# Rotary projection of the L2a attention on one core: one projection with a partner shuffle in place of two projections

## The chip, the core and the metric

The kernel runs a whole four-block decoder as one program on one core of a Trainium2 chip. The time is device microseconds of one execution, the core's first to last instruction and what lies around it. The kernel before takes 2980.1 us (median of three runs, 2977.56 to 2994.86). Most executions of a kernel agree within 0.3%, about 9 us here.

## The reference

The input `x` has 8 batches of 256 tokens with 128 features. Twelve layers are added to it one after the other: an attention, a cross attention and a feed-forward for each of four blocks. The change is in the attention code that three of them share (L0a, L2a, L3a), and above all in L2a, the only one with a rotary embedding:

```python
def _rotate_half(x):
    x1, x2 = jnp.split(x, 2, axis=-1)
    return jnp.concatenate((-x2, x1), axis=-1)

def _L2_attn_ref(x, Wq, Wkv, Wo, bo):          # 16 heads of 64, 4 key/value heads
    q = (x @ Wq).reshape(b, n, HEADS, DIM_HEAD).transpose(0, 2, 1, 3)
    kv = (x @ Wkv).reshape(b, n, 2 * KV_HEADS, DIM_HEAD)
    k = kv[:, :, :KV_HEADS].transpose(0, 2, 1, 3)
    v = kv[:, :, KV_HEADS:].transpose(0, 2, 1, 3)
    ...
    q = q * cos + _rotate_half(q) * sin
    k = k * cos + _rotate_half(k) * sin
    k = jnp.repeat(k, g, axis=1)
    v = jnp.repeat(v, g, axis=1)
    dots = jnp.einsum('bhid,bhjd->bhij', q, k) * SCALE
    attn = jax.nn.softmax(dots, axis=-1)
    out = jnp.einsum('bhij,bhjd->bhid', attn, v)
    return out.transpose(0, 2, 1, 3).reshape(b, n, HEADS * DIM_HEAD) @ Wo + bo
x = x + _L2_attn_ref(_layernorm(x, axis=-1), ...)
```

So each of the 64 values of a head needs its partner, the value 32 places away, to be rotated.

## The kernel before

`attention_rows` computes L0a, L2a and L3a. All numbers are fp32. In L2a one batch is one **pass** of eight **units** (0 to 7), and a unit is one chunk of two heads: queries and keys lie transposed, the 64 dimensions of two heads on the 128 partitions, the 256 tokens along a row (`qT`, `kT`).

A unit does, for its two heads, *scores* (PE, into `ps_s`), *max* (VectorE, `top`), *exp* (ScalarE, `probs`, four instructions of 128x256 each with a read of its accumulator), and then for earlier chunks: *turn* of the chunk before (PE transposes into `ps_p`, copied to SBUF as `probsT` by ScalarE in L2a), *inverse* of the chunk before (a small reciprocal on VectorE, widened by GpSimd into `wide`), and, for the chunk two before, *spread* (PE transposes `wide`, ScalarE copies it), *values* (PE, into `ps_o`) and *outputs* (VectorE multiplies `ps_o` by `spread` into `oT`).

Beside these, a pass makes the queries and keys of the next batch. The table `slots` says which of these **items** lie in which unit, those of the first list right after *max*, those of the second right after *inverse*. The items are the transposed input x, the queries q and keys k, the values v, the output projection y of the batch before, and the layer norm of the batch after next (ln, ln_rest). One function builds one list, `order`, from the table, and each engine walks through that same list in order and issues its part of each entry. No scheduler moves anything. All items share two PSUM banks (`ps_m`, `m_banks=2`) in turn: PE may start an item only when the item two before it has been taken out of its bank. *Scores* go round three banks (`s_banks=3`), so those of a unit wait until the first head of the unit before has been exponentiated.

A q or k item of L2a makes one chunk (8 q and 2 k items a pass). PE (line 1423) projects twice, with `w_q` and with `w_qr`, whose columns are those of `w_q` with the halves of each head exchanged, so that the partners come to lie on the same partition in the second half of the bank. VectorE (line 1301) multiplies the bank by cos and signed sin in one instruction of 128x512 into a ring of three (`turned`); GpSimd (line 1265) adds the halves into `qT` or `kT` in one instruction of 128x256. *Scores* of a batch's chunk 0 wait for all q and k items of the batch; those of later chunks have no such wait. The weights of L2a are loaded on the SyncE queue during the layer before.

Before the first pass, the same `order` runs eight units in which only items for batch 0 exist (the **prologue**). The last pass has no q, k, x or v items.

## Time and profile before

| | |
|---|---|
| time, median of three runs | 2980.1 us |
| time of the profiled execution | 2979.73 us |
| span of the profiled execution | 2977.9 us |
| PE busy over the span | 2342.9 us (79%) |
| VectorE busy | 1606.9 us (54%) |
| ScalarE busy | 1307.4 us (44%) |
| GpSimd busy | 727.4 us (24%) |
| mean granted TensorE clock | 0.861 of full |

The whole span is an average over twelve layers with different limits, so the shares of the span say little about one of them. L2a lies between 1553.6 us (its first VectorE work starts) and 1894.4 us (its last addition to `x_sb` ends). A row of the timeline gives the start of a run of like instructions, their length together, the engine, the line, the operation and the tiles; behind it, in brackets, the idle time of the engine before it and what ended that.

### The profile page before, as it was taken

How to read it: one execution, taken by the hardware profiler on the slowest of the kernel's cores; microseconds unless marked ns; L12 is line 12 of the kernel's file. 1: busy time of each engine (PE TensorE's matmuls, PEld its weight loads, DVE VectorE, ACT ScalarE, POOL GpSimd, SP SyncE). 2: the span in 40 equal slices, each digit the busy share in tenths (PEclk: the TensorE clock that was granted, in tenths of full speed). 3: DMA queues.
4: the chain of work that ended last, by engine and by line, in shares of the span. 5: the costliest groups of instructions: out<-in, count | busy, mean ns of one | idle time of the engine just before them, and what ended most of it. 6: DMA issues, size and time to landing. Idle time of an engine off the chain costs nothing. (4 is left out here: it accounts for less than half of the span.)

```text
span 2977.9 us, 49335 instructions
## 1 busy us (share of the span) xinstructions
PE 2342.9 (79%) x16238; PEld 1536.2 (52%) x16238; DVE 1606.9 (54%) x4943; ACT 1307.4 (44%) x3187; POOL 727.4 (24%) x1023
## 2 busy tenths in 40 slices
PE   6868985658887389882569999878839996899958
PEld 4624443635544244441457777557727774455533
DVE  4657772135555577753215555453337674877623
ACT  4615552124455145554426666432316553355522
POOL 0132212153332421200563332124231112222000
PEclk9969995858888578995789999988969998899979
DMA  2022224210000022213250000224410001222100
GB/s 72 2 78 83 82 58 148 46 51 29 29 29 15 30 87 74 79 32 99 71 110 1 1 1 1 75 86 150 133 44 2 1 2 39 88 77 77 37 16 14
DMA packets 130876, 160.29 MB, mean 54 GB/s; under 512 B 22581, under 2 KB 93110, under 8 KB 129478
## 3 DMA queue, kind: packets, MB, share of 16 engines
q1 hardware_dynamic: 116008, 132.90, 14.8%
q0 software_dynamic: 12016, 23.19, 3.2%
q8 instruction: 126, 2.06, 0.3%
q10 hardware_dynamic: 2624, 1.31, 0.3%
q14 instruction: 102, 0.83, 0.1%
HBM read 120.77 MB, written 36.68 MB: 53 GB/s over the span
## 5 line engine op out<-in xcount | busy, mean ns | idle before, releaser
L725 DVE CUSTOM_DVE_ANT_0 L3x_ps_ring<-L3x_ps_ring,L3x_mask_q 128x512 f32<-128x512 f32 x256 | 173.9, 708 | 65.9 <-PE L3x_ps_ring L960 51.5
L728 DVE TENSOR_REDUCE L0x_mx<-L0x_ps_ring 128x1 f32<-128x512 f32 x256 | 166.6, 685 | 70.6 <-PE L0x_ps_ring L960 69.5
L728 DVE TENSOR_REDUCE L1x_mx<-L1x_ps_ring 128x1 f32<-128x512 f32 x256 | 166.2, 685 | 61.9 <-PE L1x_ps_ring L960 61.1
L856 ACT ACTIVATE L3x_p_ring<-L3x_ps_t 128x1024 f32<-128x1024 f32 x128 | 131.1, 1025 | 144.4 <-PE L3x_ps_t L999 144.2
L856 ACT ACTIVATE L1x_p_ring<-L1x_ps_t 128x1024 f32<-128x1024 f32 x128 | 130.4, 1025 | 122.6 <-PE L1x_ps_t L992 121.8
L856 ACT ACTIVATE L0x_p_ring<-L0x_ps_t 128x1024 f32<-128x1024 f32 x128 | 130.4, 1025 | 106.8 <-PE L0x_ps_t L992 106.3
L1368 ACT ACTIVATE L2a_probs<-L2a_ps_s,L2a_top 128x256 f32<-128x256 f32 x256 | 118.0, 473 | 93.2 <-DVE L2a_top L1318 92.3
L992 PE MATMUL L3x_ps_t<-L3x_q_stack,L3x_k_stack 75*128 75x256 bf16 x512 | 123.9, 278 | 5.5 <-ACT L3x_p_ring L856 5.4
L960 PE MATMUL L1x_ps_ring<-L1x_k_stack,L1x_q_stack 72*128 72x512 bf16 x256 | 104.0, 431 | 29.7 <-DVE L1x_mx L728 16.1
L960 PE MATMUL L0x_ps_ring<-L0x_k_stack,L0x_q_stack 72*128 72x512 bf16 x256 | 103.2, 428 | 28.8 <-DVE L0x_mx L728 15.5
L999 PE MATMUL L3x_ps_t<-L3x_mask_k,const_ident_bf 128*128 128x256 bf16 x512 | 123.6, 277 | 0.0
L1368 ACT ACTIVATE L3a_probs<-L3a_ps_s,L3a_top 128x128 f32<-128x128 f32 (+1 forms) x256 | 104.2, 423 | 38.9 <-DVE L3a_top L1314 36.7
L960 PE MATMUL L3x_ps_ring<-L3x_k_stack,L3x_q_stack 72*128 72x512 bf16 x256 | 96.9, 410 | 21.1 <-DMA L3x_k_stack<-L3x_k_dram 11.6
L1318 DVE TENSOR_REDUCE L2a_top<-L2a_ps_s 128x2 f32<-128x512 f32 x128 | 82.1, 683 | 18.9 <-PE L2a_ps_s L1447 18.8
L1314 DVE CUSTOM_DVE_ANT_0 L3a_ps_s<-L3a_ps_s,const_causal_min 128x128 f32<-128x128 f32 (+1 forms) x256 | 83.8, 389 | 11.4 <-PE L3a_ps_s L1447 11.4
L1423 PE MATMUL L2a_ps_m<-L2a_xT,kept_a 128*128 128x256 f32 x320 | 88.8, 405 | 1.0 <-ACT L2a_xT L1357 1.0
L1265 POOL TENSOR_TENSOR L2a_qT<-L2a_turned 128x256 f32<-128x256 f32 x64 | 47.2, 737 | 171.9 <-DVE L2a_turned L1301 171.7
L1259 POOL COPY L3a_wide<-L3a_inverse 128x128 f32<-128x128 f32 x128 | 34.0, 295 | 225.0 <-DVE L3a_inverse L1331 225.0
L992 PE MATMUL L0x_ps_t<-L0x_q_stack,L0x_k_stack 75*128 75x256 bf16 x512 | 84.5, 292 | 5.6 <-ACT L0x_p_ring L856 5.6
L992 PE MATMUL L1x_ps_t<-L1x_q_stack,L1x_k_stack 75*128 75x256 bf16 x512 | 84.2, 291 | 5.6 <-ACT L1x_p_ring L856 5.6
L1032 PE MATMUL L1x_ps_o<-L1x_p_ring,L1x_v 128*32 128x256 f32 x1024 | 78.4, 430 | 9.2 <-ACT L1x_p_ring L856 5.5
L1032 PE MATMUL L0x_ps_o<-L0x_p_ring,L0x_v 128*32 128x256 f32 x1024 | 79.2, 434 | 5.5 <-ACT L0x_oT L863 2.1
(681 smaller groups left out, 6097.3 us busy)
## 6 DMA issues: line engine op xcount, KB each, us to landing
L0x_k_stack<-L0x_k_dram SPq DMA_DIRECT2D x96, 96.0 KB
L1x_k_stack<-L1x_k_dram SPq DMA_DIRECT2D x96, 96.0 KB
L3x_k_stack<-L3x_k_dram SPq DMA_DIRECT2D x96, 96.0 KB
L0f_w<-L0f_in_w SPq DMA_DIRECT2D x32, 256.0 KB, 7.0
L1a_rk_wide<-L1a_rk_dram SPq DMA_DIRECT2D x8, 1024.0 KB, 4.8
L1f_w<-L1f_in_w SPq DMA_DIRECT2D x32, 256.0 KB, 3.1
kept_x<-ctxT SPq DMA_DIRECT2D x24, 256.0 KB, 3.2
L0x_q_stack<-L0x_q_dram SPq DMA_DIRECT2D x96, 48.0 KB
```

The lines of the kernel that those rows point to most:

```text
L725: dve.tensor_tensor_reduce(bank, bank, mask_q[:, qt, :], 1.0, 2 * MASKED, ALU.add, ALU.max, accum_out=mx[:, qt, h:h + 1]).then_inc(took_se ...
L728: dve.tensor_reduce(mx[:, qt, h:h + 1], bank, AX, ALU.max).then_inc(took_sem(n), 1)
L856: act.activation(pr, pt, ACT.Exp, scale=scale).then_inc(exp_done.sem, 1)
L960: last = pe.matmul(out, queries[:, t * P:(t + 1) * P], keys[:, 0:seen_keys], start=True, stop=small or not masked)
L992: last = pe.matmul(out, keys[:, t * P:(t + 1) * P], queries[:, q0:q0 + nq], start=True, stop=small and not masked)
L999: last = pe.matmul(out, const["ident_bf"][:], mask_k[:, par if mask_each else 0, t, q0:q0 + nq], start=False, stop=True)
L1032: last = pe.matmul(outputs(g, par)[rows, 0, q0:q0 + nq], val, prob, start=(i == 0), stop=(i == len(pieces) - 1), skip_group_check=True)
L1265: pool.tensor_tensor(dst, part[:, 0, :], part[:, 1, :], ALU.add).then_inc(rotated, 1)
L1314: last = dve.tensor_tensor_reduce(span, span, const["causal_min"][:, S - keys_of(t):S], 1.0, -2 * MASKED, ALU.add, ALU.min, accum_out=top[ ...
L1318: dve.tensor_reduce(top[:, slot, j, :], bank.rearrange("p (t k) -> p t k", t=QT), AX, ALU.min).then_inc(top_done, 1)
L1368: last = act.activation(probs[:, n % P_RING, t, 0:keys_of(t)], ps_s[:, n % s_banks, S * t:S * t + keys_of(t)], ACT.Exp, scale=-1.0, bias=t ...
L1423: last = pe.matmul(bank[:, a * S:(a + 1) * S], lhs, xT[:], start=True, stop=True)
```

## The change

**Partners 16 partitions apart.** The 64 dimensions of a head are put in another order (`PAIRED`): dimensions 0 to 15 and 32 to 47 on its first 32 partitions, 16 to 31 and 48 to 63 on the others. The partner of each dimension is then 16 partitions away inside the same group of 32. The order is the same for queries and keys, so their products are unchanged. `w_qr` and `w_kr` go away.

**One projection, two chunks an item.** A q or k item now makes two chunks (4 q and 1 k items a pass) with the same two matmuls that made one before. VectorE multiplies the whole bank by the sine table and then by the cosine table (two instructions of 128x512 from PSUM), waits for the first of them by a semaphore, and moves the sine products to the partners' partitions with a stream shuffle of 128x512 from SBUF to SBUF. GpSimd waits for the shuffle and adds 128x512. The ring of products has two places instead of three, and so has that of the shuffled ones.

**Scores wait for their own chunk.** In all three layers *scores* wait, at every chunk, for the items with that chunk's queries and keys.

**The table of L2a** is laid out anew.

```diff
@@ GpSimd
-                        wait_taken(pool, o)
-                        dst = qT[:, b % 2, k, :] if kind == "q" else kT[:, b % 2, k, :]
-                        part = turned[:, (rotation_count[o] - 1) % 3]
-                        pool.tensor_tensor(dst, part[:, 0, :], part[:, 1, :], ALU.add).then_inc(rotated, 1)
+                        r = rotation_count[o] - 1
+                        pool.wait_ge(swap_done, r + 1)
+                        dst = (qT if kind == "q" else kT)[:, b % 2, 2 * k:2 * k + 2, :]
+                        pool.tensor_tensor(dst.rearrange("p c s -> p (c s)"), tilted[:, r % 2, 0, :], swapped[:, r % 2, :],
+                                           ALU.add).then_inc(rotated, 1)
@@ VectorE
-                        if rotation_count[o] > 3:
-                            dve.wait_ge(rotated, rotation_count[o] - 3)
-                        dve.tensor_tensor(turned[:, (rotation_count[o] - 1) % 3], item_bank(o).rearrange("p (a s) -> p a s", a=2),
-                                          angles[kind][:], ALU.mult).then_inc(took["dve"], 1)
+                        r = rotation_count[o] - 1
+                        if r >= 2:
+                            dve.wait_ge(rotated, r - 1)
+                        halves = lambda a: a.rearrange("p (c s) -> p c s", c=2)
+                        for a in (1, 0):
+                            across = angles[kind][:, a:a + 1, :].broadcast_to([P, 2, S])
+                            last = dve.tensor_tensor(halves(tilted[:, r % 2, a, :]), halves(item_bank(o)), across, ALU.mult)
+                            last.then_inc(tilt_done if a else took["dve"], 1)
+                        dve.wait_ge(tilt_done, r + 1)
+                        dve.stream_shuffle(swapped[:, r % 2, :], tilted[:, r % 2, 1, :], [(i + 16) % 32 for i in range(32)]).then_inc(swap_done, 1)
@@ PE, scores
-                        if k == 0:
-                            for what in ("q", "k"):
-                                wait_taken(pe, [i for i in items if i[0] == what and i[1] == b][-1])
-                            if rope:
-                                pe.wait_ge(rotated, max(rotation_count[i] for i in rotations if i[1] == b))
+                        c = k * RS // R
+                        needed = [[i for i in items if i[:2] == (what, b) and 2 * i[2] <= last][-1]
+                                  for what, last in (("q", c), ("k", cfg["kchunk"](c)))]
+                        for i in needed:
+                            if rope:
+                                pe.wait_ge(rotated, rotation_count[i])
+                            else:
+                                wait_taken(pe, i)
@@ slots of L2a
-   slots=[([("x",0,1)],[("k",0,1)]),([("q",0,1)],[("k",1,1)]),([("q",1,1)],[("y",0,-1)]),([("q",2,1)],[("v",0,1)]),
-          ([("q",3,1)],[("y",1,-1)]),([("q",4,1)],[("q",5,1)]),([("q",6,1)],[("ln",0,2)]),([("q",7,1)],[("ln_rest",0,2)])]),
+   slots=[([("x",0,1)],[]),([("k",0,1)],[]),([("q",0,1)],[("y",0,-1)]),([],[("v",0,1)]),
+          ([("q",1,1)],[("y",1,-1)]),([("q",2,1)],[]),([],[("ln",0,2)]),([("q",3,1)],[("ln_rest",0,2)])]),
```

What the table makes of PE's order is seen in units 5 and 6 of a pass. `L2a_ps_s` are scores, `L2a_ps_m<-L2a_xT,kept_a` a q item, `L2a_ps_p` the turns, `L2a_ps_m<-const_ident,L2a_wide` the spread, `L2a_ps_o` the values. Before:

```order
L1447 MATMUL L2a_ps_s<-L2a_kT,L2a_qT 128x256 x4
L1423 MATMUL L2a_ps_m<-L2a_xT,kept_a 128x256 x2
L1459 MATMUL L2a_ps_p<-const_ident,L2a_probs 128x128 x8
L1423 MATMUL L2a_ps_m<-L2a_xT,kept_a 128x256 x2
L1465 MATMUL L2a_ps_m<-const_ident,L2a_wide 128x128 x2
L1478 MATMUL L2a_ps_o<-L2a_probsT,L2a_v 64x256 x4
L1447 MATMUL L2a_ps_s<-L2a_kT,L2a_qT 128x256 x4
L1423 MATMUL L2a_ps_m<-L2a_xT,kept_a 128x256 x2
L1459 MATMUL L2a_ps_p<-const_ident,L2a_probs 128x128 x8
L1465 MATMUL L2a_ps_m<-const_ident,L2a_wide 128x128 x2
L1478 MATMUL L2a_ps_o<-L2a_probsT,L2a_v 64x256 x4
```

The same two units of the changed kernel:

```order
L1452 MATMUL L2a_ps_s<-L2a_kT,L2a_qT 128x256 x4
L1425 MATMUL L2a_ps_m<-L2a_xT,kept_a 128x256 x2
L1464 MATMUL L2a_ps_p<-const_ident,L2a_probs 128x128 x8
L1470 MATMUL L2a_ps_m<-const_ident,L2a_wide 128x128 x2
L1483 MATMUL L2a_ps_o<-L2a_probsT,L2a_v 64x256 x4
L1452 MATMUL L2a_ps_s<-L2a_kT,L2a_qT 128x256 x4
L1464 MATMUL L2a_ps_p<-const_ident,L2a_probs 128x128 x8
L1470 MATMUL L2a_ps_m<-const_ident,L2a_wide 128x128 x2
L1483 MATMUL L2a_ps_o<-L2a_probsT,L2a_v 64x256 x4
```

Unit 5 has one q item instead of two, and unit 6 none instead of one.

VectorE in unit 7, between its maxima and the next unit's. `L2a_turned` is the rotation before, `L2a_xn` is ln_rest, `L2a_oT` the outputs. Before:

```order
L1318 TENSOR_REDUCE L2a_top<-L2a_ps_s 128x2 x2
L1301 TENSOR_TENSOR L2a_turned<-L2a_ps_m,kept_a 128x512
L1331 RECIPROCAL L2a_inverse<-L2a_sums 128x4
L1294 TENSOR_SCALAR L2a_xn<-x_sb,L2a_mean_var,L2a_rstd 128x128 x2
L1336 TENSOR_TENSOR L2a_oT<-L2a_ps_o,L2a_spread 128x256
```

And in the changed kernel:

```order
L1323 TENSOR_REDUCE L2a_top<-L2a_ps_s 128x2 x2
L1304 TENSOR_TENSOR L2a_tilted<-L2a_ps_m,kept_a 128x512 x2
L1307 STREAM_SHUFFLE L2a_swapped<-L2a_tilted 128x512
L1336 RECIPROCAL L2a_inverse<-L2a_sums 128x4
L1293 TENSOR_SCALAR L2a_xn<-x_sb,L2a_mean_var,L2a_rstd 128x128 x2
L1341 TENSOR_TENSOR L2a_oT<-L2a_ps_o,L2a_spread 128x256
```

Three instructions of 128x512 stand where one stood. VectorE in the prologue, from the first rotation to the first maxima, before and then in the changed kernel:

```order
L1301 TENSOR_TENSOR L2a_turned<-L2a_ps_m,kept_a 128x512 x9
L1281 BN_STATS L2a_stats<-x_sb 128x6 x2
L1283 MEMSET L2a_fill 128x1
L1285 BN_AGGR L2a_mean_var<-L2a_stats 128x2 x2
L1287 TENSOR_SCALAR L2a_mean_var<-L2a_mean_var 128x2
L1301 TENSOR_TENSOR L2a_turned<-L2a_ps_m,kept_a 128x512
L1294 TENSOR_SCALAR L2a_xn<-x_sb,L2a_mean_var,L2a_rstd 128x128 x2
L1318 TENSOR_REDUCE L2a_top<-L2a_ps_s 128x2 x2
```

```order
L1304 TENSOR_TENSOR L2a_tilted<-L2a_ps_m,kept_a 128x512 x2
L1307 STREAM_SHUFFLE L2a_swapped<-L2a_tilted 128x512
L1280 BN_STATS L2a_stats<-x_sb 128x6 x2
L1282 MEMSET L2a_fill 128x1
L1284 BN_AGGR L2a_mean_var<-L2a_stats 128x2 x2
L1286 TENSOR_SCALAR L2a_mean_var<-L2a_mean_var 128x2
L1304 TENSOR_TENSOR L2a_tilted<-L2a_ps_m,kept_a 128x512 x2
L1307 STREAM_SHUFFLE L2a_swapped<-L2a_tilted 128x512
L1293 TENSOR_SCALAR L2a_xn<-x_sb,L2a_mean_var,L2a_rstd 128x128 x2
L1323 TENSOR_REDUCE L2a_top<-L2a_ps_s 128x2 x4
```

The first two rows of the second piece are the last of four such triples, so the ten rotations have become five groups of three.

## Rows read from the trace of the kernel before

**Rows 1.** Windows, pass 1: length, busy us of PE, loads, VectorE, ScalarE, GpSimd, clock.
```profile
1607.37:1647.61 40.24, 40.24 (x288) 30.01 (x287) 22.74 (x52) 26.57 (x91) 12.55 (x30) 1.00 0.01 1
```

**Rows 2.** Timeline of PE, start of units 6 and 7 of pass 3.
```profile
1719.58 1.13 PE L1447 MATMUL L2a_ps_s<-L2a_kT,L2a_qT 64*128 64x256 f32 x8
...
1723.81 1.13 PE L1447 MATMUL L2a_ps_s<-L2a_kT,L2a_qT 64*128 64x256 f32 x8
```

**Rows 3.** Timeline of pass 7: unit 0, start of unit 1, exp of unit 7.
```profile
1848.74 1.13 PE L1447 MATMUL L2a_ps_s<-L2a_kT,L2a_qT 64*128 64x256 f32 x8
1850.86 0.48 ACT L1368 ACTIVATE L2a_probs<-L2a_ps_s,L2a_top 128x256 f32<-128x256 f32 x1 [1.16 <-DVE L2a_top L1318]
1852.07 1.13 PE L1447 MATMUL L2a_ps_s<-L2a_kT,L2a_qT 64*128 64x256 f32 x8
1852.67 1.10 ACT L1379 ACTIVATE L2a_probsT<-L2a_ps_p 128x512 f32<-128x512 f32 x2
1853.62 0.42 ACT L1385 ACTIVATE L2a_spread<-L2a_ps_m 128x256 f32<-128x256 f32 x1
1854.14 0.42 DVE L1336 TENSOR_TENSOR L2a_oT<-L2a_ps_o,L2a_spread 128x256 f32<-128x256 f32 x1 [2.64 <-ACT L2a_spread L1385]
1854.48 1.28 DVE L1318 TENSOR_REDUCE L2a_top<-L2a_ps_s 128x2 f32<-128x512 f32 x2
1855.20 0.47 ACT L1368 ACTIVATE L2a_probs<-L2a_ps_s,L2a_top 128x256 f32<-128x256 f32 x1 [1.16 <-DVE L2a_top L1318]
...
1881.50 0.47 ACT L1368 ACTIVATE L2a_probs<-L2a_ps_s,L2a_top 128x256 f32<-128x256 f32 x1 [1.16 <-DVE L2a_top L1318]
```

**Rows 4.** Timeline of ScalarE, the first exp of passes 0 and 1.
```profile
1574.68 0.47 ACT L1368 ACTIVATE L2a_probs<-L2a_ps_s,L2a_top 128x256 f32<-128x256 f32 x1
...
1609.44 0.47 ACT L1368 ACTIVATE L2a_probs<-L2a_ps_s,L2a_top 128x256 f32<-128x256 f32 x1
```

**Rows 5.** Timeline of PE, start of units 2, 3 and 4 of pass 3.
```profile
1697.35 1.13 PE L1447 MATMUL L2a_ps_s<-L2a_kT,L2a_qT 64*128 64x256 f32 x8
...
1703.37 1.14 PE L1447 MATMUL L2a_ps_s<-L2a_kT,L2a_qT 64*128 64x256 f32 x8
...
1708.46 1.13 PE L1447 MATMUL L2a_ps_s<-L2a_kT,L2a_qT 64*128 64x256 f32 x8
```

**Rows 6.** Timeline of VectorE and GpSimd in unit 7 of pass 2.
```profile
1684.86 1.28 DVE L1318 TENSOR_REDUCE L2a_top<-L2a_ps_s 128x2 f32<-128x512 f32 x2
1686.06 0.68 DVE L1301 TENSOR_TENSOR L2a_turned<-L2a_ps_m,kept_a 128x512 f32<-128x512 f32 x1
1686.65 0.17 DVE L1331 RECIPROCAL L2a_inverse<-L2a_sums 128x4 f32<-128x4 f32 x1
1686.74 0.98 DVE L1294 TENSOR_SCALAR L2a_xn<-x_sb,L2a_mean_var,L2a_rstd 128x128 f32<-128x128 f32 x2
...
1686.81 0.83 POOL L1265 TENSOR_TENSOR L2a_qT<-L2a_turned 128x256 f32<-128x256 f32 x1 [2.47 <-DVE L2a_turned L1301]
```

**Rows 7.** Groups by line; behind x the count, then busy us, mean ns.
```profile
L3539 DVE TENSOR_TENSOR L1a_tail_n<-L1a_tail_n,kept_a 128x512 f32<-128x512 f32 x4 | 2.8, 692 | 0.1
L3470 POOL TENSOR_TENSOR L1a_tail_x<-L1a_tail_n,kept_a 128x512 f32<-128x512 f32 x4 | 5.1, 1266 | 0.0
```

**Rows 8.** Timeline of PE in L3a, scores of units 0 and 1 and the values before.
```profile
2286.64 0.87 PE L1478 MATMUL L3a_ps_o<-L3a_probsT,L3a_v 128*64 128x256 f32 x8
2287.44 0.93 PE L1447 MATMUL L3a_ps_s<-L3a_kT,L3a_qT 64*128 64x128 f32 x8
...
2289.54 0.87 PE L1478 MATMUL L3a_ps_o<-L3a_probsT,L3a_v 128*64 128x256 f32 x8
2290.34 0.93 PE L1447 MATMUL L3a_ps_s<-L3a_kT,L3a_qT 64*128 64x128 f32 x8
```

**Rows 9.** Timeline of VectorE in the prologue, first rotation and first max.
```profile
1559.56 0.69 DVE L1301 TENSOR_TENSOR L2a_turned<-L2a_ps_m,kept_a 128x512 f32<-128x512 f32 x1 [3.39 <-PE L2a_ps_m L1423]
...
1572.58 1.29 DVE L1318 TENSOR_REDUCE L2a_top<-L2a_ps_s 128x2 f32<-128x512 f32 x2 [0.94 <-PE L2a_ps_s L1447]
```

21 lines of the change are left out of this document (8 added, 13 removed).

## The prediction

> **What bounds the kernel now.** The page is only a start: PE is busy 79% of the span, and that is a mean over twelve layers. The change touches L2a, so I read L2a alone. First the windows, one for each pass: the steady passes are 40.24 us long and PE is busy for all of it at clock 1.00, while VectorE is busy for 22.74, ScalarE for 26.57 and GpSimd for 12.55 us [rows 1]. Then the timeline, to see what a PE unit is made of. From the scores of one unit to those of the next it is 6.02 us with a q item and a y item, 5.09 with a q and a v item [rows 5], and 4.23 with a q item alone [rows 2]. The last pass shows a unit with no item: 1852.07 - 1848.74 = 3.33 us [rows 3]. So a q or k item costs 4.23 - 3.33 = 0.90 us of PE.
>
> The last pass shows more: PE has almost no items there, and yet its exps come every 4.34 us (1855.20 - 1850.86), and from unit 0 to unit 7 they take 30.64 us [rows 3]. That is a loop over ScalarE and VectorE: exp to probsT copies 1.81, copies to spread 0.95, spread to outputs 0.52 (VectorE had been idle 2.64 us for it), outputs to max 0.34, first max to exp 0.72, together 4.34. ScalarE takes the spread after the copies, and VectorE, in order, takes the outputs before the next maxima. In a steady pass PE hides this loop; it is what is late next.
>
> **What the change takes from PE.** Five q/k items a pass instead of ten: 5 x 0.90 = 4.5 us. Unit by unit: unit 0 loses its k item and keeps x (a unit with two q/k items is 3.33 + 2 x 0.90 = 5.1, and the window's 40.24 less the other seven leaves unit 0 about 4.4, so 3.5), unit 1 keeps one item (4.23), unit 2 stays 6.02, unit 3 loses its q item (4.19), unit 4 stays 6.02, unit 5 has one (4.23), unit 6 none (3.33), unit 7 one (4.28). Sum 35.8 us. Of the gain only what lies above the 4.34 loop comes through.
>
> **What it adds on VectorE.** A rotation was one instruction whose successor starts 0.59 us later (1686.06 to 1686.65) [rows 6]. Now it is two such, 1.19 us, and a shuffle of 128x512 from SBUF to SBUF, which the trace before does not show. Bounds by rows of that shape: below, 0.59 us, the step of a PSUM multiply; above, GpSimd's 1.27 us for an SBUF operation [rows 7]. Its nearest relative is VectorE's own SBUF operation, 0.69 us [rows 7]; with a tenth for its wait on its own engine's semaphore I take 0.80. So a rotation R = 2.0 us (1.8 to 2.5), five a pass instead of ten of 0.59: 10.0 against 5.9 us.
>
> The Trainium skill, VectorE: DVE Perf Modes, section "The perf-mode tier table", gives STREAM_SHUFFLE about 2400 ns at 2048 elements and one element a cycle at best; scaled to 512 elements that is, as an estimate, 0.80 us, where fp32 tensor_tensor has 2293 ns there. The sum by it would be the same.
>
> Is there room? A unit of VectorE is maxima 1.20 (1684.86 to 1686.06), R 2.0, inverse 0.09, outputs to next max 0.34: 3.6 us, under 4.34. So the rotation sits in the 2.64 us that VectorE waited for the spread and costs nothing in units 1 and 5. Were that cover gone, each microsecond of it would be in the loop. In units 2 and 4, PE's 6.02 us cover it.
>
> **Unit 7 has no room.** It has the rotation and ln_rest. ln_rest took 0.98 us beside a GpSimd add of 0.83 us that began 0.07 us after it [rows 6]. The add grows to 128x512, 1.27 us [rows 7]. If the second half of ln_rest waits for the add to end, ln_rest grows by 0.44 to 1.42 us; if not, it stays 0.98. I take 1.42. The unit is then 1.20 + 2.0 + 0.09 + 1.42 + 0.34 = 5.05 us, 0.71 over the loop. The Trainium skill, SBUF — State Buffer, section "SBUF: two separate sides", states an exclusive lock between a VectorE operation in a 2-port mode and a GpSimd one, the later blocking wholly; by that rule ln_rest pays, and the trace agrees (two halves that touch: ln_rest ends at 1687.72, the add at 1687.64). Without the rule the time would be 3 us lower.
>
> **A steady pass after,** from exp to exp. Exps 5 to 6, 6 to 7 and 0 to 1: 3 x 4.34 = 13.02. Exp 7 to 0: 5.05. From exp 1 PE leads: to the scores of unit 2 1.21 (1852.07 - 1850.86) [rows 3], unit 2 6.02, scores to exp 1.13 + 0.72 = 1.85: 9.08. Units 3 and 4 on PE: 4.19 + 6.02 = 10.21 to exp 5 (the v copy on ScalarE hides behind unit 4). Sum 37.36 against 40.24: 2.88 us saved, in five passes (1 to 5) 14.4. Pass 6 has a q item but no ln_rest in unit 7, so 36.65 us: 3.6 saved. Pass 7 is the loop already: 0.
>
> Pass 0, exp to exp, took 1609.44 - 1574.68 = 34.76 us [rows 4]. It has no y items. After: exp 0 to 1 without copies 1.21 + 1.13 + 0.72 = 3.1; 1 to 2 on VectorE 1.20 + 2.0 + 0.1 = 3.3; 2 to 3 4.34; 3 to 4 with the v copy (0.6 more) 4.94; three of 4.34; 7 to 0 5.05. Sum 33.8: 1.0 saved.
>
> **The prologue** is VectorE's: first rotation 1559.56, first max 1572.58, 13.0 us [rows 9]. After: five rotations 10.0, layer norm about 0.9, ln_rest 1.0 to 1.4: 12.1 on average. But the first exp also waits for the x item, which waits for ln_rest. I take 0.4 saved (between 1.2 saved and 1 lost).
>
> **GpSimd.** Its add comes before the widening of the same unit in its order and is 0.5 us longer and starts 1.4 us later; PE's next spread needs the widened sums. Counted along the loop, PE waits up to 0.9 us for them, only in units after a q item and without y, where it has 4.34 - 3.33 = 1.0 us to spare. Cost 0.
>
> **Waits and loads.** Scores of L0a, L2a and L3a get one or two more waits a chunk. All of them were met long before: q3 and k3 of L3a have to be taken before PE may start the v items ahead of the scores, as the two banks demand. Does a wait that is met cost PE something? L3a's unit 0 has such waits now, the others not, and values to scores takes 0.80 us in both (2286.64 to 2287.44, 2289.54 to 2290.34) [rows 8]. Cost 0; at 0.05 us each in L3a's 56 it would be 2.8. Two weight loads fewer are issued on SyncE, a layer ahead: 0.
>
> **Sum.** 14.4 + 3.6 + 1.0 + 0.4 = 19.4 us. The profiled execution took 2979.7 us (span 2977.9), 0.4 under the median 2980.1. 2980.1 - 19.4 = 2960.7, so 2961.
>
> **Rivals.**
> 1. *The rotation is dearer than its nearest rows, but less than its cover allows to break even.* R from 2.3 to 3.0 (shuffle 1.1 to 1.8). To R = 2.7 a q unit stays within 4.34 and only unit 7, the prologue and unit 1 of pass 0 pay, about 7 us for each us of R; beyond that the five items pay everywhere, some 35 us for each. Time 2963 to 2976. For it: a wait of VectorE on itself and a new instruction. Chance 0.14.
> 2. *Slower: VectorE becomes the bound.* The same slope goes through zero near R = 3.1, a shuffle of 1.9 us, 2.7 times the 0.69 row; at 2.5 us it gives about 3000 us. For it: no row has a shuffle. Against it: every fp32 instruction of this shape on VectorE lies at 0.68 to 0.69 us. Chance 0.04.
> 3. *The loop gives way and PE stays the bound.* Pass 35.8 us in all seven: 7 x 4.4 = 31 less a little, 2950. For it: PE is what every steady window shows full. Against it: pass 7, where 30.64 us for seven units leave no slack. Chance 0.07.
> 4. *The gain is lost elsewhere, no change.* PE would idle about 1.5 us a pass and do fewer columns in the prologue; were its granted clock to fall to the lower level (1.2 GHz) for 40 us of L2a, 20 us of work would be added: 2980. Against it: 96% busy in the steady passes. Chance 0.05.
>
> My forecast, R between 1.8 and 2.3, has 0.70 and gives 2957 to 2964 with the prologue's and ln_rest's bounds. The range 2953 to 2973 adds most of rival 1 and the executions' own spread. More than 1% (29.8 us, about what a measurement of this kernel can tell) is only within rival 3: faster 0.06; slower by more than 1% needs rival 2 at its far end: 0.03; within 1%: 0.91.
>
> **What would show it.** Steady windows of L2a near 37.4 us, with PE's busy time about 36; exps 4.34 us apart from unit 5 on and 5.0 from unit 7 to 0; the idle time before exp still released by the max; shuffle near 0.8 us; ln_rest near 1.4 us; q/k matmuls 160 records instead of 320; L3a and the cross layers as long as before; the last pass the same. I am wrong in the main step if exps in units 5 to 7 come closer than 4.34 us (rival 3) or further apart with VectorE never idle (rivals 1, 2), and in the frame if L3a's passes change.

## The result and the profile after

The changed kernel took 2965.24 us, the median of 11 runs (2946.30 to 2974.38); the kernel before took 2986.19 us, the median of 11 (2968.40 to 2998.73). The ratio is 0.9939, with a 95% interval of 0.9913 to 0.9965 (the two medians alone give 0.9930). The prediction was 2961 us, within 1% of before. One execution of the experiment e6 below took 4034.32 us at a mean granted clock of 0.54 and stands in no ratio here.

| | before | after |
|---|---|---|
| span of the profiled execution, us | 2977.9 | 2963.4 |
| L2a, first layer-norm instruction of the layer to that of the next, us | 341.4 | 324.3 |
| L0a / L3a, us | 127.6 / 307.0 | 127.4 / 307.2 |
| L1a (not touched), us | 402.4 | 405.6 |
| PE busy over the span, us | 2342.9 | 2307.2 (78%) |
| VectorE busy over the span, us | 1606.9 | 1629.9 (55%) |
| mean granted TensorE clock | 0.861 | 0.859 |

The spans of the two profiles differ by 14.5 us, L2a alone by 17.1 us; L1a, which the change doesn't touch, took 3.2 us more. Layers that no kernel here touches scatter by nearly as much from one execution to the next: L0x took between 315.0 and 329.2 us, L1x between 331.8 and 342.5 us. So everything below is read from the length of L2a, which was 324.3 us in this profile and 325.2 us when the same kernel ran on another chip.

The windows of the kernel after, pass 3, pass 6 and the first seven units of pass 7, from exp to exp. The columns are the length, then busy us of PE, weight loads, VectorE, ScalarE and GpSimd, then the granted clock; the last two are the busy share and the GB/s of the DMA engines.

```profile
1688.15:1725.78 37.63, 36.00 (x269) 26.28 (x268) 25.52 (x63) 26.34 (x91) 11.79 (x24) 1.00 0.00 1
1801.02:1838.12 37.10, 36.26 (x269) 26.26 (x267) 23.36 (x55) 25.96 (x91) 10.44 (x22) 1.00 0.00 1
1838.12:1868.77 30.65, 28.55 (x221) 20.16 (x223) 12.60 (x31) 22.29 (x77) 3.74 (x14) 1.00 0.01 1
```

Against [rows 1], a steady pass lost 2.62 us, and PE is no longer busy for all of it: 36.00 of 37.63 us. The 1.63 us that it idles are one single gap, the 1.61 us ahead of the x item in the timeline below; from there to the scores of the next unit 0 PE works without a pause that the profile shows. Pass 7 stayed as it was, 30.65 us in this window [rows 3].

The timeline of the kernel after, from unit 7 of pass 3 over the boundary into pass 4. It answers [rows 6] and shows the place where the prediction and the kernel part.

```profile
1720.20 1.28 DVE L1323 TENSOR_REDUCE L2a_top<-L2a_ps_s 128x2 f32<-128x512 f32 x2
...
1720.91 0.47 ACT L1373 ACTIVATE L2a_probs<-L2a_ps_s,L2a_top 128x256 f32<-128x256 f32 x1 [1.16 <-DVE L2a_top L1323]
...
1721.39 1.28 DVE L1304 TENSOR_TENSOR L2a_tilted<-L2a_ps_m,kept_a 128x512 f32<-128x512 f32 x2
...
1722.21 1.14 PE L1452 MATMUL L2a_ps_s<-L2a_kT,L2a_qT 64*128 64x256 f32 x8
...
1722.60 0.01 DVE L1307 LOAD_MASK_SELECT L2a_swapped<-L2a_tilted  x1
1722.60 0.72 DVE L1307 STREAM_SHUFFLE L2a_swapped<-L2a_tilted 128x512 f32<-128x512 f32 x1
...
1723.22 0.16 DVE L1336 RECIPROCAL L2a_inverse<-L2a_sums 128x4 f32<-128x4 f32 x1
1723.30 1.52 DVE L1293 TENSOR_SCALAR L2a_xn<-x_sb,L2a_mean_var,L2a_rstd 128x128 f32<-128x128 f32 x2
1723.40 1.33 POOL L1263 TENSOR_TENSOR L2a_qT<-L2a_tilted,L2a_swapped 128x512 f32<-128x512 f32 x1 [4.53 <-DVE L2a_swapped L1307]
...
1724.74 0.41 DVE L1341 TENSOR_TENSOR L2a_oT<-L2a_ps_o,L2a_spread 128x256 f32<-128x256 f32 x1
1724.96 0.41 PE L1417 MATMUL L2a_ps_m<-const_ident,L2a_xn 128*128 128x128 f32 x2 [1.61 <-DVE L2a_xn L1293]
1725.07 1.27 DVE L1323 TENSOR_REDUCE L2a_top<-L2a_ps_s 128x2 f32<-128x512 f32 x2
...
1725.78 0.47 ACT L1373 ACTIVATE L2a_probs<-L2a_ps_s,L2a_top 128x256 f32<-128x256 f32 x1
...
1727.41 1.13 PE L1452 MATMUL L2a_ps_s<-L2a_kT,L2a_qT 64*128 64x256 f32 x8
...
1730.12 0.47 ACT L1373 ACTIVATE L2a_probs<-L2a_ps_s,L2a_top 128x256 f32<-128x256 f32 x1 [1.16 <-DVE L2a_top L1323]
...
1731.64 1.13 PE L1452 MATMUL L2a_ps_s<-L2a_kT,L2a_qT 64*128 64x256 f32 x8
```

VectorE works without a gap from 1720.20 to 1725.07: maxima, two multiplications, shuffle, reciprocal, ln_rest, outputs. The exps are 4.87 us apart there (1725.78 - 1720.91), and 4.34 us apart one unit later. PE stands still for 1.61 us, because the x item needs ln_rest. And the GpSimd add that completes q3 ends at 1724.73 us, while the scores of unit 0 started at 1722.21: that is possible only with the new waits.

What paces the steady pass can be followed back from the x item. Three rows of pass 3, the x item of unit 0, the scores of unit 5 and their exp:

```profile
1687.34 0.41 PE L1417 MATMUL L2a_ps_m<-const_ident,L2a_xn 128*128 128x128 f32 x2 [1.61 <-DVE L2a_xn L1293]
...
1710.33 1.14 PE L1452 MATMUL L2a_ps_s<-L2a_kT,L2a_qT 64*128 64x256 f32 x8
...
1712.22 0.47 ACT L1373 ACTIVATE L2a_probs<-L2a_ps_s,L2a_top 128x256 f32<-128x256 f32 x1 [2.28 <-DVE L2a_top L1323]
```

From the x item to the scores of unit 5 PE is busy without a gap, 22.99 us. The exp of unit 5 follows 1.89 us later, that of unit 7 another 8.69 us later, two turns of the 4.34 us loop. The next x item starts 4.05 us after that, when VectorE has done the rest of unit 7 up to ln_rest. Together that is 37.62 us, the whole pass. So the pass is paced in part by PE, in part by the loop, and in part by VectorE's unit 7, and the link that closes the ring is ln_rest to the x item.

The groups of L2a by line in the kernel after: behind x the count, then busy us and mean ns, then the idle time ahead of them.

```profile
L1304 DVE TENSOR_TENSOR L2a_tilted<-L2a_ps_m,kept_a 128x512 f32<-128x512 f32 x80 | 51.2, 681 | 4.7 <-PE L2a_ps_m L1425 4.7
L1425 PE MATMUL L2a_ps_m<-L2a_xT,kept_a 128*128 128x256 f32 x160 | 46.8, 419 | 1.9 <-DVE L2a_tilted L1304 1.2 <-ACT L2a_xT L1362 0.5
L1263 POOL TENSOR_TENSOR L2a_qT<-L2a_tilted,L2a_swapped 128x512 f32<-128x512 f32 x32 | 41.1, 1285 | 121.0 <-DVE L2a_swapped L1307 121.0
L1307 DVE STREAM_SHUFFLE L2a_swapped<-L2a_tilted 128x512 f32<-128x512 f32 x40 | 29.1, 729 | 0.0
```

Every comparison below is by the distance from the first exp of a unit to that of the next, read from ScalarE's timeline in pass 3 (in e2 the passes differ, 38.9 to 40.5 us, and in a few passes of e1 and e11 single distances differ by 0.35 us). "First exp" is its distance from the start of the layer, "behind the last" that from the exp of the last unit to the end. The latter is 12.0 to 12.1 us where the granted clock is 1.00 there and 13.2 to 13.6 where it is 0.87, before and after alike, so up to 1.6 us of a difference in L2a can be that. All in us; each row is one profiled execution.

| kernel | L2a | first exp | pass 0 | steady pass | 0-1 | 1-2 | 2-3 | 3-4 | 4-5 | 5-6 | 6-7 | 7-0 | pass 7, 0 to 7 | behind the last |
|---|---|---|---|---|---|---|---|---|---|---|---|---|---|---|
| before | 341.4 | 21.0 | 34.76 | 40.24 | 4.34 | 4.98 | 6.02 | 5.09 | 6.02 | 5.10 | 4.34 | 4.35 | 30.64 | 13.6 |
| after | 324.3 | 21.1 | 35.31 | 37.63 | 4.35 | 4.34 | 5.09 | 4.83 | 5.46 | 4.35 | 4.34 | 4.87 | 30.66 | 12.0 |
| e1_ln_unit6 | 319.7 | 18.6 | 34.49 | 37.06 | 4.34 | 4.34 | 5.08 | 4.83 | 5.46 | 4.34 | 4.33 | 4.34 | 30.62 | 13.3 |
| e2_old_waits | 343.8 | 23.1 | 38.20 | 40.04 | 4.94 | 4.34 | 5.90 | 4.83 | 5.47 | 4.34 | 4.34 | 5.88 | 30.66 | 13.2 |
| e3_shuffle_2 | 331.3 | 23.6 | 36.45 | 38.27 | 4.34 | 4.35 | 5.09 | 4.83 | 5.46 | 4.34 | 4.35 | 5.51 | 30.66 | 12.1 |
| e4_shuffle_3 | 355.6 | 27.4 | 39.03 | 41.12 | 5.14 | 4.81 | 5.44 | 4.83 | 5.46 | 4.84 | 4.34 | 6.26 | 30.65 | 13.3 |
| e5_spread_early | 329.3 | 21.2 | 35.21 | 38.87 | 3.68 | 4.23 | 6.70 | 4.19 | 6.70 | 4.23 | 4.26 | 4.88 | 28.22 | 12.1 |
| e6_reordered | 312.7 | 18.5 | 33.20 | 36.94 | 3.54 | 4.23 | 4.23 | 7.14 | 4.23 | 4.24 | 5.10 | 4.23 | 27.29 | 12.1 |
| e7_projection_2 | 350.1 | 24.3 | 37.83 | 40.96 | 4.34 | 4.35 | 6.80 | 4.84 | 6.32 | 5.10 | 4.34 | 4.87 | 30.66 | 12.1 |
| e8_before_new_waits | 342.0 | 21.0 | 37.26 | 40.19 | 4.34 | 4.95 | 6.02 | 5.09 | 6.02 | 5.10 | 4.33 | 4.34 | 30.62 | 12.0 |
| e9_y_before_v | 307.0 | 18.6 | 32.91 | 36.02 | 3.54 | 4.23 | 4.23 | 6.22 | 4.23 | 4.23 | 5.11 | 4.23 | 27.30 | 12.1 |
| e10_changed_again | 325.2 | 21.1 | 36.14 | 37.63 | 4.35 | 4.34 | 5.09 | 4.83 | 5.46 | 4.35 | 4.34 | 4.87 | 30.66 | 12.1 |
| e11_old_waits_q3_in_6 | 322.7 | 22.4 | 34.90 | 37.06 | 4.34 | 4.34 | 5.08 | 4.83 | 5.46 | 4.34 | 4.34 | 4.33 | 30.61 | 12.1 |

### The profile page after: what moved, and what is told of

Same layout as the page of the kernel before. It is cut to its first block and busy times, and to the rows that moved or that the text cites. A ratio compares the mean times of both kernels' runs of the same rounds, so it can differ in the third digit from the quotient of the medians.

```text
span 2963.4 us, 49078 instructions
## 1 busy us (share of the span) xinstructions
PE 2307.2 (78%) x16045; PEld 1507.7 (51%) x16078; DVE 1629.9 (55%) x5023; ACT 1306.0 (44%) x3187; POOL 721.6 (24%) x983
## 5 line engine op out<-in xcount | busy, mean ns | idle before, releaser
L958 PE MATMUL L0x_ps_ring<-L0x_k_stack,L0x_q_stack 72*128 72x512 bf16 x256 | 103.2, 428 | 28.8 <-DVE L0x_mx L726 15.5
L2172 DVE TENSOR_TENSOR L2f_hid<-L2f_gated,L2f_ps 128x256 f32<-128x256 f32 (+1 forms) x93 | 38.8, 420 | 75.0 <-ACT L2f_gated L2217 75.0
L1341 DVE TENSOR_TENSOR L2a_oT<-L2a_ps_o,L2a_spread 128x256 f32<-128x256 f32 x64 | 27.1, 424 | 95.4 <-ACT L2a_spread L1390 83.2
```

The source lines that it names most:

```text
L958: last = pe.matmul(out, queries[:, t * P:(t + 1) * P], keys[:, 0:seen_keys], start=True, stop=small or not masked)
L2172: dve.tensor_tensor(hid[0:rows, n % 2, i, :], gated[0:rows, m % H_RING, :], h_bank(m)[0:rows, TILE:2 * TILE], ALU.mult).then_inc(h_out, 1)
```

## The experiments

The theory at the start: the gain is PE's work alone; it stops at the 4.34 us loop over ScalarE and VectorE; and unit 7, with rotation and ln_rest in a row, costs more than the loop. The main rival was that the steady pass after the change is still PE's, with its idle time spread anywhere. e4 and e6 to e8 ran on a second chip, e9 to e11 on a third; on both, L1f and L2f took about 20 us longer each, in every kernel (before: 3028.15 and 3031.12 us), while the steady passes of L2a are the same (37.63 us in e10 as after the change, 40.19 us in e8 against 40.24 us before).

### e1: ln_rest out of unit 7

```diff
-   slots=[([("x",0,1)],[]),([("k",0,1)],[]),([("q",0,1)],[("y",0,-1)]),([],[("v",0,1)]),
-          ([("q",1,1)],[("y",1,-1)]),([("q",2,1)],[]),([],[("ln",0,2)]),([("q",3,1)],[("ln_rest",0,2)])]),
+   slots=[([("x",0,1)],[]),([("k",0,1)],[]),([("q",0,1)],[("y",0,-1)]),([],[("v",0,1),("ln",0,2)]),
+          ([("q",1,1)],[("y",1,-1)]),([("q",2,1)],[]),([],[("ln_rest",0,2)]),([("q",3,1)],[])]),
```

> The changed kernel with ln_rest taken out of unit 7 (where it stands behind the rotation of q3) into unit 6, and ln into unit 3. Theory: in the changed kernel unit 7 costs 0.52 us over the 4.34 us loop (exp to exp 4.87), and the late end of ln_rest makes PE wait 1.6 us for the x item, which delays the scores of unit 2 by 0.31 us more. Both go: steady pass 37.62 to 36.8 us, L2a 324.3 to about 319.5 us. Its two operations no longer lie beside the GpSimd add, so they take 0.49 us each (mean) instead of 0.74. Rival (the pass is set by PE's work alone, 35.96 us busy of 37.62, the rest being spread everywhere): the pass stays at 37.6 and L2a at 324.

Measured: L2a 319.7 us, steady pass 37.06 us, exp 7 to exp 0 4.34 us. The first timeline row below is ln_rest, now without a GpSimd add beside it, the second PE in unit 0.

```profile
1709.93 0.57 DVE L1293 TENSOR_SCALAR L2a_xn<-x_sb,L2a_mean_var,L2a_rstd 128x128 f32<-128x128 f32 x2
...
1718.08 0.41 PE L1470 MATMUL L2a_ps_m<-const_ident,L2a_wide 128*128 128x128 f32 x2 [0.69 <-POOL L2a_wide L1257]
```

Unit 7's excess over the loop is gone in full (0.53 us). Of the second part, 0.31 us, hardly anything came: PE no longer waits for the x item, but 0.69 us for GpSimd's widening right behind it, so the scores of unit 1 come little earlier. So a pass gained 0.57 us where 0.83 was expected. The rival, a pass that stays at 37.6 us, falls. That L2a came out as expected all the same, 4.6 us less, is made of other parts: 3.3 us in passes 0 to 6, 2.5 in the prologue, which the expectation left out (first exp 18.6 us after the layer's start, not 21.1), and 1.3 lost behind the last exp, to the lower clock. In the prologue of the kernel after, the x item stands behind the last ln_rest, and ScalarE, in order, copies x and loads its table before the first exp:

```profile
1575.90 0.39 ACT L1362 ACTIVATE L2a_xT<-L2a_ps_m 128x256 f32<-128x256 f32 x1 [10.42 <-PE L2a_ps_m L1417]
1576.31 1.28 ACT L1373 ACT_TABLE_LOAD   x1
1577.60 0.47 ACT L1373 ACTIVATE L2a_probs<-L2a_ps_s,L2a_top 128x256 f32<-128x256 f32 x1
```

The first maxima had started at 1574.98 us there, 2.62 us before the exp. In e1 the x item comes earlier, and the exp starts 0.70 us after the first maxima.

Alone, the two halves of ln_rest take 0.57 us together. They took 0.98 us beside an add of 0.83 us [rows 6] and 1.52 us beside one of 1.33 us: what ln_rest pays follows the length of the add. It's the second half that pays: in the kernel after it ends about 0.1 us after the add in every pass that has an ln_rest. The expectation of 0.49 us each was still too high; one lasts 0.33.

### e2 and e8: the waits alone, undone and added

e2 is the changed kernel with the old waits:

```diff
-                        c = k * RS // R
-                        needed = [[i for i in items if i[:2] == (what, b) and 2 * i[2] <= last][-1]
...
+                        if k == 0:
+                            for what in ("q", "k"):
+                                wait_taken(pe, [i for i in items if i[0] == what and i[1] == b][-1])
+                            if rope:
+                                pe.wait_ge(rotated, max(rotation_count[i] for i in rotations if i[1] == b))
```

> The changed kernel with the old waits in all three layers: unit 0 waits for every query and key of its pass, the other units for none. Theory: the rotation of q3 lies in unit 7 and its GpSimd add ends 2.5 us after the scores of unit 0 start now (1724.73 against 1722.21), so the scores of unit 0 come 2.5 us later, its exp about 0.8 us later and the x item 0.9 us later: steady pass 38.5 us instead of 37.62, L2a about 331 us instead of 324.3, L3a 307 us and L0a 127.4 us as before. Rival (the wait at unit 0 is met in either form, as the prediction had it): L2a 324.3. Rival (each wait costs PE a little): L3a shorter by 1 to 3 us.

Measured: L2a 343.8 us, 19.5 us more than after and 2.4 us more than before; L3a 307.0 and L0a 127.9 us. The timeline of e2 at the boundary of passes 4 and 5, and the window of the four microseconds behind it:

```profile
1766.60 1.33 POOL L1263 TENSOR_TENSOR L2a_qT<-L2a_tilted,L2a_swapped 128x512 f32<-128x512 f32 x1 [4.53 <-DVE L2a_swapped L1307]
...
1768.13 1.53 PE L1449 MATMUL L2a_ps_s<-L2a_kT,L2a_qT 64*128 64x256 f32 x8 [2.65 <-issue]
1769.59 0.69 PE L1417 MATMUL L2a_ps_m<-const_ident,L2a_xn 128*128 128x128 f32 x2
...
1770.07 1.91 PE L1461 MATMUL L2a_ps_p<-const_ident,L2a_probs 128*128 128x128 f32 x8
```

```profile
1768.10:1772.30 4.20, 4.17 (x22) 3.29 (x22) 1.61 (x4) 1.98 (x8) 1.50 (x5) 0.59 0.00 0
```

PE stands still for 2.65 us until the add of q3 has ended at 1767.93 us, as the theory said (2.5). What it left out is the second half of the cost: behind that gap the granted clock is 0.59 over four microseconds, and the eight turning transposes take 1.91 us in place of 1.04. That isn't so behind each gap. PE stands still for 2.60 to 2.74 us at all seven boundaries of passes; the lower clock follows at four of them (1609, 1689, 1768 and 1808 us) and not at the other three, for one of which the gap and the window behind it are:

```profile
1650.52 1.13 PE L1449 MATMUL L2a_ps_s<-L2a_kT,L2a_qT 64*128 64x256 f32 x8 [2.66 <-issue]
```

```profile
1650.50:1654.70 4.20, 4.18 (x34) 3.13 (x36) 1.61 (x4) 2.64 (x11) 1.50 (x5) 1.00 0.01 4
```

The steady passes are 38.9 to 40.5 us long instead of the 38.5 expected. The mechanism held, its price was more than twice the expected 7 us. Of the 19.5 us, 2.0 lie before the first exp, 2.9 in pass 0, 13.4 in passes 1 to 6 and 1.2 behind the last exp, where the clock was 0.87; that last part need not come from the waits. Both rivals fall: the wait is not met in either form, and L3a, where 56 units lose two waits each, is not shorter.

e8 is the kernel before with the per-chunk waits alone (the same lines as in the change, with one item for each chunk in L2a).

> The kernel before with the per-chunk waits alone, in all three layers. Theory: there PE is busy in all of a steady pass of L2a, nothing waits for the rotations, so the waits bring nothing by themselves: L2a 341 to 342 us, pass 40.24 us, L3a 307 us, L0a 127.6 us. Rival (each wait that is met costs PE something): L3a and L2a longer by 1 to 3 us. Rival (the waits bring a gain alone): L2a under 340 us.

Measured: L2a 342.0, L3a 306.8, steady pass 40.19 us. Its window, as [rows 1]:

```profile
1712.64:1752.83 40.19, 40.19 (x288) 29.93 (x287) 22.75 (x53) 26.52 (x91) 12.51 (x28) 1.00 0.00 1
```

Alone, the waits bring nothing and cost nothing. Together with e2 this is the clearest result of the study: the new waits are worth about 0 in the kernel before and 18 to 19.5 us in the kernel after.

### e11: old waits, q3 one unit earlier

```diff
-   slots=[([("x",0,1)],[]),([("k",0,1)],[]),([("q",0,1)],[("y",0,-1)]),([],[("v",0,1)]),
-          ([("q",1,1)],[("y",1,-1)]),([("q",2,1)],[]),([],[("ln",0,2)]),([("q",3,1)],[("ln_rest",0,2)])]),
+   slots=[([("x",0,1)],[]),([("k",0,1)],[]),([("q",0,1)],[("y",0,-1)]),([],[("v",0,1),("ln",0,2)]),
+          ([("q",1,1)],[("y",1,-1)]),([("q",2,1)],[]),([("q",3,1)],[]),([],[("ln_rest",0,2)])]),
```

with the waits of e2.

> The changed kernel with the old waits (unit 0 waits for all queries and keys of its pass), the q3 item moved from unit 7 to unit 6, ln to unit 3 and ln_rest alone in unit 7. Theory: the old waits cost 19.5 us in e2 only because q3's rotation ended 2.5 us after the scores of the next unit 0 could start; a unit earlier it is done in time, so the per-chunk waits are not needed: steady pass 37.0 us, L2a 319 to 321 us. Rival (the old waits cost something by themselves, or by another rotation): L2a above 325 us.

Measured: steady pass 37.06 us, L2a 322.7 us. The pass is that of e1, so the passes behave as the theory has it; the layer is 1.7 us above the upper end, since the first exp comes 22.4 us after the start, 3.8 us later than in e1. There the old wait still costs: the first scores of the prologue wait for the GpSimd add of the last query, and the x item, behind them on PE, comes late as well.

```profile
1603.95 2.08 PE L1449 MATMUL L2a_ps_s<-L2a_kT,L2a_qT 64*128 64x256 f32 x8 [4.57 <-POOL L2a_qT L1263]
```

The granted clock up to the first exp is 0.65 (0.78 in e1), and these scores take 2.08 us instead of the 1.14 of e1, so a part of the 3.8 us is the clock. So in the passes the old waits hurt through one item alone, the query that is projected last before the boundary; in the prologue they cost something in either place (in e2 the first exp comes 2.0 us later than after the change).

### e3 and e4: a dearer rotation

```diff
+                        for again in range(1):
+                            if r * 1 + again:
+                                dve.wait_ge(spare_done, r * 1 + again)
+                            dve.stream_shuffle(spare[:], tilted[:, r % 2, 1, :], [(i + 16) % 32 for i in range(32)]).then_inc(spare_done, 1)
                         dve.stream_shuffle(swapped[:, r % 2, :], tilted[:, r % 2, 1, :], [(i + 16) % 32 for i in range(32)]).then_inc(swap_done, 1)
```

The lines that make the spare tile and its semaphore are left out. e4 has range(2) and r * 2.

> The changed kernel with a second shuffle into a spare tile in every rotation, nothing left out. VectorE's rotation grows from 1.83 to about 2.45 us (2.55 at most). Theory: only unit 7, the prologue and unit 1 of pass 0 pay, about 7 to 11 us for each us of rotation: steady pass 38.24 us, exp 7 to exp 0 5.5 us, exps of units 5 to 7 still 4.34 us apart, L2a about 331 us. Rival (VectorE is the bound everywhere): five rotations a pass pay, 3 us a pass, L2a about 346 us. Rival (VectorE has slack everywhere): L2a 324 us.

Measured: exp 7 to 0 5.51, steady pass 38.27, L2a 331.3 us. VectorE's timeline of a rotation in e3:

```profile
1708.73 1.28 DVE L1306 TENSOR_TENSOR L2a_tilted<-L2a_ps_m,kept_a 128x512 f32<-128x512 f32 x2
...
1709.93 0.72 DVE L1312 STREAM_SHUFFLE L2a_spare<-L2a_tilted 128x512 f32<-128x512 f32 x1
...
1710.56 0.75 DVE L1313 STREAM_SHUFFLE L2a_swapped<-L2a_tilted 128x512 f32<-128x512 f32 x1
1711.18 0.18 DVE L1342 RECIPROCAL L2a_inverse<-L2a_sums 128x4 f32<-128x4 f32 x1
```

The rotation takes 2.45 us, 0.62 more than the 1.83 of after, and nothing but unit 7, the prologue and pass 0 became longer. That is 7.0 us for 0.62 us, 11 us for each microsecond. Both rivals fall.

> The changed kernel with two more shuffles into a spare tile in every rotation: the rotation grows from 1.83 to about 3.1 us, by 0.64 us for each shuffle as with one more. The prediction put its break-even there: 'through zero near R = 3.1', that is an L2a of about 341 us, as before the change. Theory, counted unit by unit: a VectorE unit with a rotation is 1.20 + 3.11 + 0.10 + 0.34 = 4.75 us, so exp 1 to 2 and 5 to 6 grow from 4.34 to 4.75 and exp 7 to 0 from 5.51 (one more shuffle) to 6.15, while the units with y (5.09 and 5.46) still cover it: pass 39.7 us, L2a 342 to 345 us. Rival (only unit 7 and the prologue pay, as with one more): L2a 338 us.

Measured: L2a 355.6 us, outside the expected 342 to 345 and far from the prediction's break-even. VectorE's rotation of unit 7 and PE's x item behind it, from two timelines of e4, and the window behind:

```profile
1711.73 1.28 DVE L1306 TENSOR_TENSOR L2a_tilted<-L2a_ps_m,kept_a 128x512 f32<-128x512 f32 x2
...
1714.94 0.17 DVE L1342 RECIPROCAL L2a_inverse<-L2a_sums 128x4 f32<-128x4 f32 x1
```

```profile
1716.69 0.41 PE L1423 MATMUL L2a_ps_m<-const_ident,L2a_xn 128*128 128x128 f32 x2 [2.10 <-DVE L2a_xn L1295]
1716.94 1.61 PE L1470 MATMUL L2a_ps_p<-const_ident,L2a_probs 128*128 128x128 f32 x8
```

```profile
1717.00:1719.00 2.00, 2.00 (x13) 1.67 (x13) 1.15 (x3) 1.86 (x8) 1.15 (x3) 0.56 0.00 0
```

The rotation is 3.21 us. The units that were counted came out as counted: 1-2 and 5-6 at 4.81 and 4.84 (4.75), 7-0 at 6.26 (6.15). Not counted: PE now stands still for 2.10 us before the x item, and then the granted clock is 0.56, the turning takes 1.61 us instead of 1.04, and exp 0 to 1 grows to 5.14 and 2 to 3 to 5.44. Of the 2.85 us by which the pass is longer than in e3, 1.71 us lie in the three distances that were counted (1-2, 5-6, 7-0) and 1.15 us in those two; how much of the 1.15 us is the late x item and how much the clock wasn't separated. The pass is 41.1 us instead of 39.7. So the kernel breaks even below R = 3.1, somewhere between 2.45 (L2a 331.3) and 3.21 us (355.6).

### e7: PE's work put back

```diff
-                        for a in range(2):
+                        for a in range(2) if not rope else (0, 1, 0, 1):
```

> The changed kernel with each query and key projection of L2a computed twice into the same bank, so that PE has the old count of projection matmuls while VectorE and GpSimd stay as after the change; nothing is left out. Theory: what the change gained is PE's work alone, so PE is the bound again: pass near 40.3 us with PE busy for nearly all of it, L2a 341 to 346 us. Rival (the gain came from the order of the items or from the waits): pass about 37.6 us, L2a 324 us.

Measured: steady pass 40.96, L2a 350.1 us. The window of its pass 3:

```profile
1720.54:1761.50 40.96, 40.21 (x289) 30.07 (x288) 26.01 (x63) 26.55 (x91) 11.76 (x24) 1.00 0.01 1
```

With the old number of projection matmuls the whole gain is gone, and PE is again busy for nearly all of the pass. The layer is longer than before, by 8.7 us, and above the expected range: exp 7 to 0 is 4.87 instead of 4.35, as in the kernel after, the first exp comes 3.3 us later, and pass 0 is 3.1 us longer (it is 2.5 us longer in e8 too, where the rotations are those of before). That the longer rotations are the price is likely, but no run separates it from the new order of the items. The rival, a gain by the order or by the waits alone, falls.

### e5, e6, e9 and e10: the loop taken away

In e5 the spread item stands before the turning in L2a:

```diff
         put("exp", b, part)
+        if cfg.get("spread_early") and ends(u - 2):
+            put("spread", *divmod((u - 2) // GROUPS, C))
         if not cfg.get("turn_early"):
             put("turn", *divmod(u - 1, U))
...
-            for kind in ("spread", "values", "outputs"):
+            for kind in ("values", "outputs") if cfg.get("spread_early") else ("spread", "values", "outputs"):
```

> The changed kernel with the spread item of L2a put between exp and turn: on ScalarE it goes ahead of the two probsT copies, on PE ahead of the turning; nothing else moves. Theory: the 4.34 us loop (exp, copies 1.81, spread 0.95, outputs 0.52, max 0.34, exp 0.72) loses the 0.95 us of the copies. ScalarE's work in a unit, 3.45 us, is then the floor in pass 7, which goes from 30.65 to about 24.4 us from unit 0 to unit 7; steady passes become PE's, 36.0 to 36.6 us instead of 37.62; L2a 307 to 311 us instead of 324.3. Rival (the 4.34 us come from elsewhere, PE's own order or the banks of the scores): passes 37.6 and 30.65 us, L2a 324 us.

Measured: L2a 329.3 us, 5.0 slower than after. Two windows of e5, a steady pass and pass 7, and PE in unit 2, with the outputs behind:

```profile
1673.54:1712.41 38.87, 36.59 (x268) 26.25 (x267) 26.08 (x63) 26.33 (x91) 11.72 (x24) 1.00 0.00 1
1828.42:1856.60 28.18, 28.03 (x221) 20.00 (x222) 12.80 (x31) 22.29 (x77) 3.72 (x15) 1.00 0.01 1
```

```profile
1683.27 2.05 PE L1495 MATMUL L2a_ps_m<-L2a_w_o,L2a_oT 128*128 128x128 f32 x16 [0.37 <-DVE L2a_tilted L1306]
...
1686.38 0.42 DVE L1343 TENSOR_TENSOR L2a_oT<-L2a_ps_o,L2a_spread 128x256 f32<-128x256 f32 x1 [0.73 <-PE L2a_ps_o L1485]
```

The 4.34 us loop is gone: in pass 7 units without a y item follow each other in 3.37 us, and PE is busy for all but 0.15 us of that pass. So in pass 7 the loop was what the prediction took it for. But pass 7 takes 28.22 us, not the 24.4 expected: ScalarE isn't the next floor there, PE is. The steady pass even became longer, and that half of the theory failed. A unit with q and y took 6.70 us: the three items rotation, spread, y share two banks, so y waits for the rotation, and the rotation waits for the maxima of the same unit; scores, maxima, rotation, y and values became one chain over PE and VectorE.

e6 keeps the lines of e5 and takes these waits away:

```diff
         put("max", b, part)
+        if cfg.get("spread_early") and ends(u - 1):
+            put("inverse", *divmod((u - 1) // GROUPS, C))
...
-        if ends(u - 1):
+        if not cfg.get("spread_early") and ends(u - 1):
...
-          slots=[([("x",0,1)],[]),([("k",0,1)],[]),([("q",0,1)],[("y",0,-1)]),([],[("v",0,1)]),
-          ([("q",1,1)],[("y",1,-1)]),([("q",2,1)],[]),([],[("ln",0,2)]),([("q",3,1)],[("ln_rest",0,2)])]),
+          slots=[([("x",0,1)],[]),([("k",0,1)],[]),([("q",0,1)],[]),([],[("v",0,1),("ln",0,2),("y",0,-1)]),
+          ([("q",1,1)],[]),([("q",2,1)],[]),([],[("ln_rest",0,2),("y",1,-1)]),([("q",3,1)],[])]),
```

> The changed kernel with four moves in L2a: the spread item ahead of the turning (as in e5), the reciprocal ahead of the rotation, so that GpSimd widens before its rotation add, ln_rest in unit 6, and both y items in units without a rotation (3 and 6). Theory: e5 broke the 4.34 us loop (exps 3.37 us apart in pass 7) but lost 2 x 0.7 us a pass in the units with q and y, where y's bank of the items is the one that the rotation before it has still to read, 0.9 us for the widening and 0.6 us for the x item. Without these the steady pass is PE's 36.0 to 36.5 us, pass 7 about 28 us from unit 0 to 7, L2a 309 to 314 us, against 324.3 after the change and 341.4 before; ratio to the kernel before about 0.990. Rival (another loop over the engines waits behind each of these): passes above 37 us, L2a above 320 us.

Measured: L2a 312.7 us, pass 7 27.29 us, ratio to before 0.990 (0.9861 to 0.9940). The steady pass is 36.94 us, over the expected 36.5, and the timeline names the difference:

```profile
1755.08 2.05 PE L1497 MATMUL L2a_ps_m<-L2a_w_o,L2a_oT 128*128 128x128 f32 x16 [0.91 <-ACT L2a_spread L1394]
```

With v ahead of y in unit 3, y's bank is that of the spread. e9 puts v behind y:

```diff
-          ([],[("v",0,1),("ln",0,2),("y",0,-1)])
+          ([],[("ln",0,2),("y",0,-1),("v",0,1)])
```

> The kernel of e6 with the first y item put ahead of the v item in unit 3, nothing else. Theory: in e6 PE waited 0.91 us a pass there, since the y item uses the bank that the spread of the same unit still had to be read from; now the v item comes two items after the spread, 2 us later. Pass 36.05 us instead of 36.95, L2a 306 to 308 us instead of 312.7, ratio to the kernel before 0.987 to 0.989. Rival (the v item or ScalarE's copy of it waits instead): L2a stays at 312 to 313 us.

Measured: L2a 307.0 us, ratio to before 0.9873 (0.9852 to 0.9894). The window of a steady pass:

```profile
1740.55:1776.57 36.02, 36.02 (x269) 26.32 (x268) 25.29 (x63) 26.38 (x91) 11.98 (x23) 1.00 0.01 2
```

PE is busy for all of it again. This kernel is 1.3% faster than the kernel before. It differs from the changed kernel in several moves at once, so what each of them brings isn't shown, only their sum. On the same chip the changed kernel itself gave this:

> The changed kernel once more, on the chip of this call: L2a should again be 324.3 us within 1 us and its steady passes 37.6 us, whatever the rest of the program takes; ratio to the kernel before 0.991 to 0.997 as measured.

Measured: ratio 0.9916 (0.9895 to 0.9938), L2a 325.2 us, steady pass 37.63 us. The intervals of e9 and e10 do not overlap, if only just.

## Why the prediction was right, and where it was not

**The size.** It forecast 19.4 us less, a ratio of 0.9935; 0.9939 was measured. In the two profiles L2a lost 17.1 us, by parts: passes 1 to 5 13.1 (forecast 14.4), pass 6 3.1 (3.6), pass 0 -0.6 (+1.0), the prologue -0.1 (+0.4), pass 7 0 (0), and 1.6 us behind the last exp, which was not forecast and does not come from the change: the clock there was 0.87 in the one profile and 1.00 in the other, and e8, with the old projections, has 12.0 us there like the kernel after. So the change itself is worth 15.5 us in these profiles, a fifth less than forecast; that the ratio came out within 0.0004 of the forecast is in part luck, in the scatter of the other layers and in the clock behind the last exp. The two rows, before and after:

```profile
1881.50:1895.10 13.60, 9.79 (x66) 7.24 (x62) 2.59 (x9) 5.04 (x15) 1.06 (x4) 0.87 0.01 1
```

```profile
1868.50:1880.80 12.30, 8.51 (x68) 6.39 (x64) 2.86 (x9) 4.93 (x15) 1.07 (x4) 1.00 0.01 2
```

**PE's work and the loop: right.** PE has 36.0 us in a pass (35.8), exps 5-6, 6-7 and 0-1 are 4.35, 4.34 and 4.35 us (4.34), and pass 7 stayed. e7 shows that PE's work was the gain, e5 that the loop sets pass 7. In a steady pass two turns of the loop stand in the ring of 37.62 us; e5, which breaks the loop alone, doesn't show what they cost there, since PE and VectorE then waited for each other elsewhere. Rival 3 falls: the exps of units 5 to 7 came no closer than 4.34 us.

**The rotation: right, a little too dear.** R was 1.83 us (2.0): the shuffle lasts 0.73 us as a mean, and its successor starts 0.62 us after it (0.80). The prediction had taken a length, 0.69 us, for a step; on VectorE a step is about 0.1 us shorter than the length (0.59 against 0.68 in [rows 6]). A wait of VectorE on itself ahead of it, for which a tenth was allowed, adds nothing that the rows show. The Trainium skill's table in VectorE: DVE Perf Modes, section "The perf-mode tier table", scaled to 512 elements, gave 0.80 us as an estimate; the trace has 0.73. That estimate takes off 1536 elements at one a cycle; in straight proportion the table's 2400 ns would give 0.60.

**Unit 7: right.** 4.87 us (5.05), with ln_rest at 1.52 us (1.42). Its terms are those written down, and the shuffle was shorter. e1 shows the mechanism: alone ln_rest takes 0.57 us. The Trainium skill, SBUF — State Buffer, section "SBUF: two separate sides", has a VectorE operation in a 2-port mode and a GpSimd one exclude each other; by that rule ln_rest ends after the add, and the traces agree (1724.82 against 1724.73 us, and with the shorter add of [rows 6] 0.08 us after it too). A sharing of the ports that merely slowed both isn't seen: the add takes 1.33 us beside ln_rest and 1.27 us elsewhere.

**The step that failed: "From exp 1 PE leads".** The prediction let PE be ready 1.21 us behind exp 1, and gave exps 1 to 5 19.29 us. They take 19.72 (4.34 + 5.09 + 4.83 + 5.46), since the scores of unit 2 come 1.52 us behind exp 1. PE's unit 0 was put at 3.5 us as if the x item could start at once; it waits 1.61 us for ln_rest, the unit is 5.20 us long, and PE has no lead to give. That wait is all of PE's idle time in a pass. The 0.71 us over the loop that unit 7 was charged with was only VectorE's side of a late ln_rest; PE's side was left out. It is 0.31 of the 0.43 us; the rest is that the y unit is 6.11 us long, not 6.02, and 0.04 us from scores to exp.

**Pass 0: 35.31 us, not 33.8.** 1.8 us of it are in the first two units (3.98 and 4.19 us against 3.1 and 3.3). The window of the kernel after:

```profile
1577.60:1583.00 5.40, 4.23 (x14) 3.03 (x15) 1.40 (x3) 3.36 (x15) 0.00 (x0) 0.50 0.00 0
```

The granted clock is 0.50, the lower level (1.2 GHz), after a prologue in which PE was busy 9.82 of 21.10 us; before, it was busy 15.05 of 20.98, and the clock behind it 0.78. The prediction counted pass 0 with durations at full clock. Whether the clock there is lower because of the change was not settled: e8, with PE busy 15.8 us in the prologue, had 0.56, and its pass 0 took 37.26 us. The first two units together took 7.42 us before and 9.94 us in e8, which has the same work there, and 8.17 us after and 9.00 us in e10, the same kernel again. So they scatter by as much as the change could have cost.

**The prologue: 0.1 us longer, not 0.4 shorter,** inside its bounds of 1.2 saved and 1 lost. What the prediction named as the risk, a first exp that waits for the x item, is what happened (2.62 us from the first maxima to the first exp).

**GpSimd.** Cost 0 is right for the changed kernel, but not because PE has time to spare: the widening hides behind the late x item. Where that is gone, in e1, PE waits 0.69 us for the widening in unit 0, the only gap left in its pass of 37.06 us.

**The waits: the cost right, their worth not asked.** The cost was put at 0, and e8 shows 0. But the prediction treated this part of the change as one that does nothing, and it never asked what the old wait would cost in the new order. q3's rotation ends 2.5 us after the scores of unit 0 start. With the old waits L2a is 343.8 us and there is no gain at all (e2). All durations for this stood in the prediction: rotation 2.0, add 1.27, unit 4.3.

**The rivals.** Rival 1's slope of 7 us for each us of R was too low: 11 (e3). Six passes and five rotations in the prologue make 11 by themselves; the prologue's were left out of the slope, though its own part had them. The break-even near R = 3.1 was too high (e4): the low slope puts it too far, and PE's longer wait for the x item, with the lower clock behind it, was not in the sum. Rival 4, a fall of the clock in the steady passes, did not happen after the change; it did in e2 and e4.

## What to carry to other kernels

When work is taken from the bound engine, look at once for the loop that it hid, and at every item that the engine will now reach earlier than its input is there: here that was the x item behind ln_rest and the last query behind its rotation. A wait for everything that is harmless while the engine is late can cost the whole gain once it is early, so reordering items and narrowing waits belong together, and what they are worth shows only when each is taken back from the finished kernel. And when a loop is broken by moving one item ahead, follow the ring of banks: who used the bank two items before, and when is it read?

## What was not expected of the hardware

- PE's granted clock can fall after a short stand-still. After gaps of 2.65 us (e2) and 2.10 us (e4) it was 0.59 over 4.2 us and 0.56 over 2 us, and eight transposes took 1.91 and 1.61 us instead of 1.04. It fell behind all six gaps of 2.09 to 2.11 us in e4, but only behind four of the seven of 2.60 to 2.74 us in e2, so the length of the gap alone doesn't decide; what else does stays open. After gaps of 1.61 to 1.70 us (after), 0.91 us (e6) and 0.69 us (e1) the passes stayed at 1.00. In e2 L2a became 19.5 us longer, where the gap alone had been put at 7.
- A shuffle across partitions takes hardly longer than another SBUF operation of its size on VectorE: 0.73 us for 128x512 against 0.69 [rows 7], and the mask load that goes with it takes 0.01 us.
- ln_rest on VectorE took 0.57, 0.98 or 1.52 us. What differed was only what GpSimd did beside it: nothing, an add of 0.83 us, or an add of 1.33 us.
